# Quantised layer: the third layer's raw query weights are asked for in four groups behind the folding loads of pairs one to four

## The chip, the cores and the metric

The kernel runs on one core of one Trainium2 chip. The metric is the device time in microseconds; the kernel before has a median of 2282.21 us over 3 runs (2281.89 to 2282.95).

## The reference

A chain of four layers, each a gated cross-attention and a gated feed-forward part, on x of 16 x 56 tokens of width 256 (896 tokens, 7 tiles of 128) with a context of 16 x 1500 x 64:

```python
x = x + tanh(g_xattn[n]) * Ln_xattn(layernorm(x), ctx, Wq, w_kc_q, w_kc_kv, W_qr, W_kr, Wo)
x = x + tanh(g_ffn[n]) * Ln_ffn(layernorm(x), ...)
```

The change lies in the feed-forward part of the second layer (n = 1), the quantised one, and concerns weights of the attention of the third (n = 2):

```python
def _L1_ffn_ref(x, w_gate, w_up, w_down, ln_weight):      # bit_linear: x to 8 bits per row, w to -1, 0, 1
    h = silu(bit_linear(x, w_gate)) * bit_linear(x, w_up)  # 896 x 1024
    h = rms_norm(h, ln_weight)
    return bit_linear(h, w_down)

def _L2_xattn_ref(...):                                    # 16 heads, K = 128, D_CQ = 192, R = D_C = 64
    q_hk = (hidden_q @ Wq.T).reshape(Bv, Sv, H, K)
    q_big = apply_rope(einsum('bshk,hkq->bshq', q_hk, w_kc_q))
    q_r = einsum('bshq,hqr->bhsr', q_big, W_qr)
    k_r = einsum('bld,hdr->bhlr', kv_r, W_kr)
    ...
    ctx_lat = einsum('bhsd,hkd->bhsk', ctx_c, w_kc_kv)
    return ctx @ Wo.T
```

## The kernel before

The program is cut into stages that end with a meeting of all five engines (`stage_end`). Each layer is an attention stage, a projection and a feed-forward stage. Inside a stage each engine runs its own program in order and waits on semaphores of the others. SyncE (SP) has no arithmetic: it issues the loads, in the order of its program, and a wait in it holds every load behind it.

The feed-forward stage of the quantised layer works by one list of tasks, `FFN1`, that all engines walk. Its main part goes over the 7 token tiles ("blocks"): `qin` (VectorE, DVE, quantises a tile of the input, L2454), `in` (TensorE, PE, turns it, L1639; ScalarE, ACT, copies it, L2037), `hidden` (PE: gate and up products through the helper at L922; ACT: silu of the gate, `sg`, L2047; DVE: product with up, `h`, L2778), `square` (ACT, L2052; then GpSimd, POOL, multiplies h by `ln_w`, L2237), `rms` (DVE L2792, POOL L2241), `quant` (DVE: maximum L2797, small steps, quantising of h L2454), `turn` (PE L1658, ACT L2057), `down` (PE L922, DVE adds to X, L2783).

Woven into it is the folding of the third layer's weights, head pair by head pair (8 pairs of 2 heads): `fload` (SP: WrT, then WoT and Wv), `fu` (PE, L1181, 8 products; ACT copies to U2, L1709) and `fm` (PE, L1187; ACT to MH, L1712; DVE to ML, L2298). `fold_order(2, 1)` has one set of buffers for the three weights of a pair, so the load of pair p + 1 waits for the products of pair p: SP waits for `fu` of pair p ahead of WrT, and for `fm` of pair p ahead of WoT and Wv. `bit_order` puts `fu` and `fm` of one pair at the end of each block. Thus PE's order in round k is: hidden of block k, down of k - 3, turn of k - 2, in of k + 2, fu and fm of pair k.

The other loads of the stage are issued in `sp_bits`: `ln_w`, the folding loads of pair 0, then eight large ones, `Wq2` (4 x 512 KB) and `Wc2` (4 x 384 KB), the raw query weights and w_kc_q of the third layer in four groups of 4 heads; a group counts on its own semaphore, `heads_in(g)`. Then come the folding loads of pairs 1 to 7. PE waits for `heads_in(g)` in the next stage only, in `pe_rope_queries`, ahead of heads 0, 4, 8 and 12.

Of the kernel before, what the change touches and what calls it, by code (L numbers as in the profile page):

```python
# [432 lines left out]
def build(nc, io, out, steps=8):  # L433
# [494 lines left out]
    def stage_end(e, n):  # L928

        e.drain().then_inc(meet.sem, 1)  # L930
        e.wait_ge(meet.sem, 5 * n)
# [43 lines left out]
    def sp_fold(e, n, p):  # L975
        src = lambda name: io[f"a{n}_{name}"][:, 2 * p:2 * p + 2]
        q = p - FOLD_BUFS[n]
        buf = fold_bufs[n][p % FOLD_BUFS[n]]
        if q >= 0:
            e.wait_ge(*fu_made.at(n, q))  # L980
        e.dma_start(buf["wr"][:, :, :], src("WrT")).then_inc(fold_r.sem(n, p), 16)
        if q >= 0:
            e.wait_ge(*fm_made.at(n, q))
        e.dma_start(buf["wo"][:, :, :], src("WoT")).then_inc(fold_m.sem(n, p), 16)
        e.dma_start(buf["wv"][:, :, :], src("Wv")).then_inc(fold_m.sem(n, p), 16)
        if n == 2:
            return
        if q >= 0:
            e.wait_ge(*fa_made.at(n, q))
        e.dma_start(buf["wq"][:, :, :], src("Wq")).then_inc(fold_a.sem(n, p), 16)  # L990
        e.dma_start(buf["wc"][:, :, :, :], src("WcT")).then_inc(fold_a.sem(n, p), 16)
# [128 lines left out]

    def sp_bits(e):
        e.dma_start(lw[:, :], io["f1_ln"].rearrange("(a n) -> a n", a=1).broadcast_to([P, I1])).then_inc(ln_in.sem(), 16)
        begun = False
        for kind, *t in FFN1:
            if kind == "fload":
                sp_fold(e, *t)
            elif not begun:
                begun = True
                for g in range(4):
                    hs = slice(4 * g, 4 * g + 4)  # L1130
                    e.dma_start(Wq2[g // 2][:, 4 * (g % 2):4 * (g % 2) + 4, :], io["a2_Wq"][:, hs, :]).then_inc(heads_in.sem(g), 16)
                    e.dma_start(Wc2[:, hs, :], io["a2_Wc"][:, hs, :]).then_inc(heads_in.sem(g), 16)
        stage_end(e, next(met))
# [8 lines left out]
    def sync_program(e):  # L1142
        e.dma_start(ident[:, :], io["ident"]).then_inc(ident_in.sem(), 16)
        e.dma_start(X[:, :, :], io["x"].rearrange("b s d -> (b s) d").rearrange("(i p) d -> p i d", p=P)).then_inc(x_in.sem(), 16)
        e.dma_start(gates[:, 0:4], io["g_xattn"].rearrange("(a n) -> a n", a=1).broadcast_to([P, 4])).then_inc(g_in.sem(), 16)
        e.dma_start(gates[:, 4:8], io["g_ffn"].rearrange("(a n) -> a n", a=1).broadcast_to([P, 4])).then_inc(g_in.sem(), 16)
        for tile, name in ((Wq0, "a0_Wq"), (Wk0, "a0_Wk")):
            for r in range(4):
                e.dma_start(quarter(tile, r), heads_of(name, r)).then_inc(fold0_a.sem(), 16)
        e.dma_start(V0[:, :, :], io["ctx"][:, 0:S, :].rearrange("b l d -> l b d")).then_inc(v0_in.sem(), 16)  # L1150
        e.dma_start(mtf[:, :], io["mask_t"]).then_inc(masks_in.sem(), 16)
        e.wait_ge(*fold0_m.at())
        e.wait_ge(*fold0_a.at())
        for k, name in enumerate(("f1_gate", "f1_up", "f1_down")):
            e.dma_start(raws[k][:, :], io[name]).then_inc(wraw_in.sem(k), 16)
        stage_end(e, next(met))
        for n in range(4):
            sp_attention(e, n)
            if n == 1:
                sp_bits(e)  # L1160
            else:
                sp_experts(e, n)
        e.wait_ge(*x_stored.at())
# [1745 lines left out]
```

## Time and profile before

| | us |
|---|---|
| median of 3 runs | 2282.21 |
| profiled execution, first to last instruction (span) | 2276.6 |
| PE busy | 2145.4 |
| DVE busy | 1540.0 |
| POOL busy | 1482.0 |
| ACT busy | 1036.5 |
| feed-forward stage of the quantised layer, first load to first load of the next stage | 861.3 to 932.8 |

Times in the rows are microseconds from the start of the span. A row of a timeline has: start, duration, engine, line of the kernel, operation, output<-input, shape, how many were merged (x), and in brackets the idle time ahead of it with what ended it. PEld is the load of weights into PE. SPq is SP's queue: a row there is the issue of a transfer, not the transfer. A row of stretches has: from:to, length, busy time of PE, PEld, DVE, ACT and POOL with the number of instructions, the TensorE clock that was granted (1.00 is 2.4 GHz, 0.50 is 1.2 GHz), the mean busy share of the 16 DMA engines, and the GB/s that they moved.

### The profile page before, as it was taken

To read this page: it belongs to the slowest core of one execution; us is meant where nothing else is said; L and a number is where in the kernel's file an instruction comes from. 1 tells how busy PE (TensorE), PEld (TensorE's weight loads), DVE (VectorE), ACT (ScalarE), POOL (GpSimd) and SP (SyncE) were. 2 spreads that over 40 slices of the span, in tenths; PEclk is the share of its full clock that TensorE was granted. 3 is DMA by queue.
4 is the path that set the end of the run, shared out by engine and by line. 5 is a ranking of instruction groups with operands and counts; after the bars stand their busy time and mean duration, and the time that the engine had idled before them with its cause. 6 is when DMAs were issued, how large, how long until landed. Compare 5 with 4: busy or idle time off the path is not lost.

```text
span 2276.6 us, 30620 instructions
## 1 busy us (share of the span) xinstructions
PE 2145.4 (94%) x11236; PEld 1519.8 (67%) x11236; DVE 1540.0 (68%) x2492; ACT 1036.5 (46%) x1533; POOL 1482.0 (65%) x933
## 2 busy tenths in 40 slices
PE   7797999999999997898999999979998999999988
PEld 5585777766666664565666666578896666666588
DVE  6766863588888856666787888653335787888653
ACT  4452333555555445212555545434335555545443
POOL 0355763488888873465888888724443888888744
PEclk9798999999999998898999999989999999999989
DMA  3126875211121104001111111025531111111022
GB/s 93 44 74 190 254 239 148 74 42 41 41 61 42 28 29 131 24 1 42 41 42 61 41 41 43 6 84 150 145 85 55 41 42 60 41 42 43 6 65 82
DMA packets 60640, 160.14 MB, mean 70 GB/s; under 512 B 9669, under 2 KB 19669, under 8 KB 60108
## 3 DMA queue, kind: packets, MB, share of 16 engines
q1 hardware_dynamic: 60108, 157.86, 23.2%
q8 instruction: 90, 1.47, 0.3%
q14 instruction: 58, 0.48, 0.1%
q10 hardware_dynamic: 384, 0.33, 0.1%
HBM read 143.18 MB, written 14.98 MB: 69 GB/s over the span
## 4 chain that ended last, share of the span: by engine, by line
PE 83%; DVE 6%; ACT 3%; issue 2%; POOL 2%; DMA 2%; SPq 1%; ACTq 0%; PEldq 0%; DVEq 0%; POOLq 0%; PEld 0%
PE psum L922 21%; PE psum L1426 19%; PE psum L1416 10%; PE psum L1397 10%; PE psum L1418 10%; PE psum L1580 2%; PE psum L1443 2%; PE psum L1537 2%; PE psum L1303 1%; PE psum L1181 1%; POOL CL L1871 1%; DMA WqrT<-in_a_WrT 1%; PE psum L1201 1%; PE psum L1277 1%; ACT E L1849 0%
## 5 line engine op out<-in xcount | busy, mean ns | idle before, releaser
L1849 ACT ACTIVATE E<-psum 125x896 f32<-125x896 f32 x576 | 528.1, 920 | 574.4 <-PE psum L1418 546.9
L2417 DVE TENSOR_REDUCE mx<-psum 128x1 f32<-128x500 f32 x945 | 611.8, 675 | 166.5 <-PE psum L1397 164.5
L2151 POOL TENSOR_TENSOR SA<-SA,E 125x896 f32<-125x896 f32 x282 | 597.4, 2118 | 22.1
L1426 PE MATMUL psum<-E,V 125*64 125x448 f32 x2304 | 472.0, 544 | 0.0
L1416 PE MATMUL psum<-Q,K 128*125 128x448 f32 x1152 | 332.1, 369 | 2.3 <-ACT E L1849 2.3
L1397 PE MATMUL psum<-K,Q 128*128 128x500 f32 x945 | 328.8, 402 | 2.6 <-ACT Q L1836 2.2
L1418 PE MATMUL psum<-Q,K 128*125 128x448 f32 x1152 | 330.3, 368 | 0.0
L1426 PEld LDWEIGHTS psum<-E,V 125*64 125x64 f32 x2304 | 171.6, 136 | 213.9 <-issue 202.5
L2151 POOL TENSOR_TENSOR SA<-SA,SB 125x896 f32<-125x896 f32 x93 | 194.2, 2088 | 148.5 <-DVE SB L2440 148.5
L1397 PEld LDWEIGHTS psum<-K,Q 128*128 128x128 f32 x945 | 174.5, 188 | 134.3 <-issue 34.7
L1416 PEld LDWEIGHTS psum<-Q,K 128*125 128x125 f32 x1152 | 213.2, 187 | 37.0 <-ACT E L1849 6.9
L1418 PEld LDWEIGHTS psum<-Q,K 128*125 128x125 f32 x1152 | 214.8, 186 | 21.8
L2202 POOL TENSOR_TENSOR HL<-HF,HH 128x448 fp32r<-128x448 f32 x70 | 81.2, 1163 | 135.7 <-ACT HH L1957 135.7
L2444 DVE RECIPROCAL RS<-psum 128x448 f32<-128x448 f32 x48 | 142.0, 2958 | 25.4 <-PE psum L1443 25.4
L2440 DVE TENSOR_TENSOR SB<-E,E 125x896 f32<-125x896 f32 x96 | 121.2, 1262 | 28.4 <-ACT E L1849 28.4
L2659 DVE TENSOR_TENSOR HF<-R,psum 128x448 f32<-128x448 f32 x62 | 38.4, 621 | 139.2 <-PE psum L922 122.5
L2151 POOL TENSOR_TENSOR SA<-E,E 125x896 f32<-125x896 f32 x48 | 102.2, 2129 | 46.5 <-ACT E L1849 46.5
L2212 POOL TENSOR_SCALAR S<-slot_of_t,slots 128x896 fp32r<-128x896 bf16 x32 | 91.5, 2864 | 46.3 <-DMA slot_of_t<-slots_scratch 32.1
L2132 POOL TENSOR_TENSOR Q<-QR,Q 64x448 fp32r<-64x448 f32 x96 | 109.5, 1141 | 11.9 <-POOL SA L2151 7.1
L1836 ACT ACTIVATE Q<-QR 64x448 fp32r<-64x448 f32 x192 | 110.5, 575 | 3.7 <-ACTq L930 0.3
L922 PE MATMUL psum<-YH,WH 128*128 128x448 f32 x264 | 104.4, 395 | 2.4 <-DVEq L930 2.4
L922 PE MATMUL psum<-YL,WH 128*128 128x448 f32 x264 | 100.2, 380 | 0.0
(299 smaller groups left out, 3591.5 us busy)
## 6 DMA issues: line engine op xcount, KB each, us to landing
K<-kt_scratch SPq DMA_DIRECT2D x48, 750.0 KB, 4.8
K<-kt_scratch SPq DMA_DIRECT2D x48, 375.0 KB, 6.0
EW<-in_f_w SPq DMA_DIRECT2D x64, 256.0 KB, 8.3
kt_scratch<-kt SPq DMA_DIRECT2D x16, 750.0 KB, 7.7
WS<-in_f_w SPq DMA_DIRECT2D x31, 384.0 KB, 4.6
GB<-gates_scratch SPq DMA_DIRECT2D x36, 224.0 KB, 3.9
slot_of_t<-slots_scratch SPq DMA_DIRECT2D x64, 112.0 KB, 4.8
WoT<-in_a_WoT SPq DMA_DIRECT2D x24, 256.0 KB, 4.2
```

The lines of the kernel that those rows point to most:

```text
L922: i = e.matmul(o, a, b, start=start and n == 0, stop=stop and n == len(pairs) - 1, **kw)
L1397: e.matmul(psum[:, bank, 0:CW], Q1n[b % 3][:, tok(j)], K1t[b % 3][:, c * CW:(c + 1) * CW], start=True, stop=True).then_inc(small_made.sem, 1)
L1416: e.matmul(psum[0:LP, pair + c, 0:HT], K1t[b % 3][:, cols], Q1n[b % 3][:, half[c]], start=True, stop=False)
L1418: i = e.matmul(psum[0:LP, pair + c, 0:HT], K2t[b % 2][:, cols], Q2n[b % 2][:, half[c]], start=False, stop=True)
L1426: i = e.matmul(psum[c * DC:(c + 1) * DC, 4 + b % 2, 0:HT], V[0:LP, b, k * DC:(k + 1) * DC], E[g[n, b, k] % NE][0:LP, half[c]], start=k == ...
L1836: i = e.activation(high, raw, ACT.Copy)
L1849: e.activation(E[m % NE][0:LP, :].rearrange("p (c q) -> p c q", c=2), psum[0:LP, pair:pair + 2, 0:HT], ACT.Exp).then_inc(exp_set.sem, 1)
L2132: e.tensor_tensor(low, raw, high.bitcast(F32), ALU.subtract).then_inc(*(pool_own.up() if odd == 0 else (q2_set.sem, 1)))
L2151: e.tensor_tensor(SA[b % 2][0:LP, :], a[0:LP, :], x[0:LP, :], ALU.add).then_inc(sum_set.sem, 1)
L2417: e.tensor_reduce(mx[:, b % 2, j * 3 + c:j * 3 + c + 1], psum[:, bank, 0:CW], AX.X, ALU.max).then_inc(small_free.sem, 1)
L2440: e.tensor_tensor(SB[list(PAIRED).index(k)][0:LP, :], e0, e1, ALU.add).then_inc(pair_set.sem, 1)
L2444: e.reciprocal(RS[:, :], psum[:, bank, 0:HT]).then_inc(small_free.sem, 1)
```

## The change

SP's walk over `FFN1` still issues the folding loads at the same tasks. The large loads are no longer issued all at once at the first task that is no `fload` (behind pair 0). Group g of them (one `Wq2` and one `Wc2` load) is issued directly behind the folding loads of pair p = g + 1, so behind pairs 1, 2, 3 and 4. Transfers, sizes, buffers and semaphores are the same.

```diff
     def sp_bits(e):
         e.dma_start(lw[:, :], io["f1_ln"].rearrange("(a n) -> a n", a=1).broadcast_to([P, I1])).then_inc(ln_in.sem(), 16)
-        begun = False
         for kind, *t in FFN1:
             if kind == "fload":
-                sp_fold(e, *t)
-            elif not begun:
-                begun = True
-                for g in range(4):
+                n, p = t
+                sp_fold(e, n, p)
+                g = p - 1
+                if 0 <= g < 4:
                     hs = slice(4 * g, 4 * g + 4)
                     e.dma_start(Wq2[g // 2][:, 4 * (g % 2):4 * (g % 2) + 4, :], io["a2_Wq"][:, hs, :]).then_inc(heads_in.sem(g), 16)
                     e.dma_start(Wc2[:, hs, :], io["a2_Wc"][:, hs, :]).then_inc(heads_in.sem(g), 16)
```

## Rows read from the trace of the kernel before

**Rows 1.** The page: its first line, and the chain that ended last by engine.

```profile
span 2276.6 us, 30620 instructions
PE 83%; DVE 6%; ACT 3%; issue 2%; POOL 2%; DMA 2%; SPq 1%; ACTq 0%; PEldq 0%; DVEq 0%; POOLq 0%; PEld 0%
```

**Rows 2.** Three stretches of the quantised layer's stage; columns as told above.

```profile
861.00:869.00 8.00, 6.12 (x22) 3.26 (x22) 3.24 (x12) 3.53 (x5) 0.00 (x0) 0.57 0.83 258
869.00:878.00 9.00, 2.90 (x17) 1.40 (x16) 4.96 (x12) 3.08 (x6) 2.90 (x2) 0.85 0.95 339
878.00:932.00 54.00, 41.58 (x256) 26.92 (x256) 41.72 (x103) 30.61 (x62) 23.26 (x26) 0.87 0.17 52
```

**Rows 3.** Timeline of SP: the last large load, then pair 1's WrT and Wv.

```profile
867.12 0.43 SPq L1132 DMA_DIRECT2D Wc<-in_a_Wc  x1
...
869.12 0.48 SPq L981 DMA_DIRECT2D WqrT<-in_a_WrT  x1
...
870.27 0.43 SPq L985 DMA_DIRECT2D Wv<-in_a_Wv  x1
```

**Rows 4.** Issue to landing: WrT pairs 0-1, WrT 2-7, Wv 2-7, Wc's four.

```profile
DMA to landing us min/median/max: 5.1/6.8/8.6
...
DMA to landing us min/median/max: 2.6/2.7/2.9
...
DMA to landing us min/median/max: 2.5/2.7/3.3
...
DMA to landing us min/median/max: 5.9/7.8/10.0
```

**Rows 5.** Timeline of PE (L1639 in, L1181 fu, L1187 fm, L1658 turn, L922 hidden).

```profile
871.34 0.38 PE L1639 MATMUL psum<-ident,Y 128*128 128x128 f32 x2
877.82 1.51 PE L1181 MATMUL psum<-WqrT 64*96 64x64 f32 x8 [6.10 <-DMA WqrT<-in_a_WrT]
...
882.96 1.04 PE L1658 MATMUL psum<-ident,h 128*128 128x128 f32 x8
...
884.15 0.89 PE L1181 MATMUL psum<-WqrT 64*96 64x64 f32 x8
884.97 0.65 PE L1187 MATMUL psum<-WoT,Wv 128*64 128x256 f32 x4
885.55 1.90 PE L922 MATMUL psum<-wq,xqT 128*128 128x512 bf16 x8
...
889.85 0.89 PE L1181 MATMUL psum<-WqrT 64*96 64x64 f32 x8 [0.44 <-DVE X L2783]
...
905.61 1.14 PE L1181 MATMUL psum<-WqrT 64*96 64x64 f32 x8 [0.54 <-DVE X L2783]
```

**Rows 6.** Timeline of ACT: silu of blocks 2 and 3.

```profile
882.24 1.12 ACT L2047 ACTIVATE sg<-psum,c_gate 128x1024 f32<-128x1024 f32 x1 [0.39 <-PE psum L922]
...
886.98 1.10 ACT L2047 ACTIVATE sg<-psum,c_gate 128x1024 f32<-128x1024 f32 x1
```

**Rows 7.** Timeline of DVE: quantising of blocks 0, 1, 2 (L2454), h of 2, 3 (L2778).

```profile
875.89 0.75 DVE L2454 TENSOR_SCALAR h<-h,h_scale 128x1024 f32<-128x1024 f32 x1
...
883.39 1.28 DVE L2778 SCALAR_TENSOR_TENSOR h<-psum,c_up,sg 128x1024 f32<-128x1024 f32 x1 [2.12 <-ACT sg L2047]
...
887.08 0.75 DVE L2454 TENSOR_SCALAR h<-h,h_scale 128x1024 f32<-128x1024 f32 x1
...
888.12 1.28 DVE L2778 SCALAR_TENSOR_TENSOR h<-psum,c_up,sg 128x1024 f32<-128x1024 f32 x1
...
893.26 2.50 DVE L2454 TENSOR_SCALAR h<-h,h_scale 128x1024 f32<-128x1024 f32 x1
```

**Rows 8.** Timeline of POOL: multiplication by ln_w of blocks 2 and 3.

```profile
887.16 2.90 POOL L2237 TENSOR_TENSOR h<-h,ln_w 128x1024 f32<-128x1024 f32 x1 [1.76 <-ACT sg L2052]
...
892.87 2.34 POOL L2237 TENSOR_TENSOR h<-h,ln_w 128x1024 f32<-128x1024 f32 x1 [0.64 <-ACT sg L2052]
```

**Rows 9.** A stretch behind block 5's start; columns as in rows 2.

```profile
906.00:909.00 3.00, 3.00 (x14) 1.30 (x14) 2.79 (x13) 1.82 (x5) 1.24 (x3) 0.52 0.17 49
```

## Prediction of what the change does to the time

> **What bounds the kernel now.** I read the page first: the span is 2276.6 us, and TensorE (PE) holds 83% of the chain that ended last [rows 1]. The median of the three runs is 2282.21 us, 5.6 us more than this span; the edit touches nothing outside the span, so I work out a difference and take it from the median. Then the three stretches of the quantised layer [rows 2]: in 861 to 869 us the DMA engines are 83% busy, in 869 to 878 us 95% busy while PE works 2.90 of 9 us, and in the remaining 54 us they are 17% busy. So the stage has one place where transfers rule. The queue of SyncE (SP) shows why [rows 3]: the last of the eight large loads goes out at 867.12, and only behind it, at 869.12, the first folding load of pair 1 (WqrT). It lands 8.6 us later, where the six of pairs 2 to 7, which have a quiet queue, take 2.6 to 2.9 [rows 4]. PE, which runs its program in order, ends its last step at 871.34 + 0.38 = 871.72 and stands 6.10 us until that load is there; the profile names it as the releaser [rows 5].
>
> Ahead of this point nothing moves: pair 1's first load waits for the product of pair 0, which PE ends at 869.1 in either version, and pair 0's loads already stand in front of the large ones. The large loads themselves (3.5 MB) are first read in the next stage, behind 932 us, so they have slack of tens of microseconds.
>
> **The change, part by part.**
>
> *Removed: the eight issues between the loads of pairs 0 and 1.* Pair 1's first load goes out at 869.12 as now, since it waits for PE, but now nothing is left in front of it. It then lands at 869.12 + 2.6 to 2.9 = 871.7 to 872.0 [rows 3, 4]. Released 0.1 us after the landing, as now (877.82 against 869.12 + 8.6), its product "fu" starts at about 871.9 instead of 877.82: 5.9 us earlier on PE. The second product of the pair, "fm", starts 0.82 us behind it when warm (884.97 against 884.15) [rows 5], so 872.75; but its last load (Wv, issued at 870.27) takes 2.5 to 3.3 us, median 2.7, and lands at 872.8 to 873.6 [rows 3, 4]. I take 873.1 for fm.
>
> *The clock of PE comes back too.* The stop makes PE restart at half speed: pair 1's fu takes 1.51 us, pair 2's 0.89 [rows 5], and from its start to the ScalarE (ACT) activation of the next block (sg) it is 882.24 - 877.82 = 4.42 us instead of 886.98 - 884.15 = 2.83 [rows 5, 6]: 1.6 us more. Stop and restart together would let block 2 go 5.9 + 1.6 = 7.5 us earlier. That isn't what the stage gains, because VectorE (DVE) becomes late.
>
> *What is late next: DVE and GpSimd (POOL) in block 0's quantising.* DVE quantises block 0 at 875.89, by its own chain, which doesn't move. Now it takes 0.75 us, beside an idle POOL. In block 2 it takes 2.50 [rows 7]: POOL had begun its multiplication by ln_w at 892.87, 0.39 us before DVE's 893.26, and DVE ends at 893.26 + 2.50 = 895.76, 0.55 us after POOL's end at 892.87 + 2.34 = 895.21 [rows 7, 8]. DVE has three such rows (2.2 to 2.6 us) among its seven blocks. Where DVE was first (887.08 against 887.16) DVE keeps its 0.75 and POOL takes 2.90 instead of 2.34. After the change POOL's multiplication of block 1 starts 3.01 us behind fu (887.16 against 884.15), plus what fm is held: 871.9 + 3.01 + 0.35 = 875.3. That is 0.6 us ahead of DVE's 875.89, so DVE should be held: POOL ends at 877.65, DVE at 878.2 instead of 876.64. From there to its product of the next block (h) it needs 0.3 us, with a small copy between (888.12 against 887.08 + 0.75), so h of block 2 starts at 878.5 instead of 883.39 [rows 7]: 4.9 us earlier. Beside this, the Trainium skill ("GPSIMD Engine Reference", section Specifications) says that the two engines share their SBUF interfaces, with contention where a DVE instruction uses two ports; the rows 7 and 8 agree. Without that rule the time would be that of rival A, with it that of my forecast.
>
> *The next block.* PE turns block 0's quantised rows 0.15 us after DVE's end: 878.35, and starts pair 2's fu 1.19 us behind that (884.15 against 882.96): 879.54 [rows 5]. Its sg follows 2.83 us later, 882.37, and lasts 1.12 [rows 6], so h of block 3 can start at 883.5; DVE's own chain, 4.73 us from h to h (888.12 against 883.39), would give 883.2 [rows 7]. So 883.5 against 888.12: 4.6 us earlier. From here each block is a copy of the one before: fu of pair 3 waits for DVE's X (0.44 us) [rows 5], and DVE moves along.
>
> *Added: four times two large loads behind pairs 1 to 4.* Group 0 goes out from 870.75, directly behind Wv. The queue is free from then on: fu of pair 1 ends at about 872.8 and releases pair 2's first load. A group is 896 KB, at the 339 GB/s of the saturated stretch 2.7 us [rows 2], so group 0 is through by about 874.5 and pair 2's first load lands by 877.3 at the latest, 2.2 us ahead of its use at 879.54. Pairs 3 to 5 have longer blocks around them (893.26 - 887.08 = 6.2 us and more from one quantising to the next [rows 7]) and so more slack. An issue takes SP about 0.4 us [rows 3], on a queue that waits for PE anyway: nothing. The last group goes out near 888 us, some 40 us ahead of need: nothing. The waits of SP are the old ones; none is added. So this part is priced 0, with bounds of 0 and of the second rival's price; a gain is excluded because no transfer of this stage is wanted earlier than now, except those of pair 1.
>
> *What takes some back.* With DVE held, PE has nothing from 875.6 (fm at 873.1, block 2's products 0.58 behind it and 1.90 long [rows 5]) to 878.35, and then only small work until block 3's products, 1.40 us behind fu, at 880.9. In the profile the clock is 0.85 of full over the stretch with the long stop and 0.87 over the rest of the stage [rows 2]: pair 5's fu at 905.61 takes 1.14 us and the granted clock is 0.52 in 906 to 909 [rows 5, 9], after a block in which PE had stood for DVE, while in the blocks of pairs 2 and 3 fu takes the warm 0.89. So after such short stops it falls in some blocks only; I take every other. If it falls here, sg of block 3 comes up to 1.6 us later, and some 1.2 if fu has already begun. Half of 1.2, 0.6, goes off: 4.6 - 0.6 = 4.0. Later falls move about in either direction (a slow fu lets DVE go ahead of POOL and saves the 2.50 - 0.75 = 1.75 us of a collision), which I leave at 0 with 1 us to each side.
>
> Sum: 4.0 us, 2282.2 - 4.0 = 2278.2 us.
>
> **The rivals.**
>
> *A. No collision in block 0.* If Wv lands 3.3 us after its issue, the top of its range, fm is 0.5 us later still and POOL starts at 875.8 to 875.9, level with DVE's 875.89. From there on DVE goes first and ends at 876.64. PE turns block 0 at 876.8, fu of pair 2 comes at 878.0, sg at 880.8, h of block 3 at 882.0 instead of 888.12: 6.1 us earlier. Less 0.3 for the clock, 5.8: 2276.4. For it: only 0.6 us separate the two, and large loads follow directly behind Wv. Against: the median landing of 2.7.
>
> *B. The folding loads still wait, now for the group ahead.* If every group held the next pair's load by what the load of pair 1 takes now (8.6 us; the large ones themselves take up to 10.0 [rows 4]), fu of pairs 2 to 5 would follow each other by 8.6 + 0.9 = 9.5 us: 871.9 + 4 x 9.5 = 909.9 for pair 5, against 905.61 now [rows 5], 4.3 us slower, 2286.5. It decides from an average landing of (905.61 - 871.9) / 4 - 0.9 = 7.5 us. Against: 8.6 us came with eight loads in front, not two, and a block's length passes after each group. This is also where the Trainium skill ("DMA: Bandwidth & Descriptors", section Queues, rings and completion order) speaks against the change: each engine consumes a ring's descriptors in order, so a load behind a group waits for all of it. By the row of pair 1 that is true; by my rates it costs no more than the slack.
>
> *C. The gain is mostly given back.* A clock fall in block 2 and one more collision, of block 1 (POOL and DVE were 0.08 us apart there), cost 1.6 and 1.75: 4.6 - 3.3 = 1.3, 2280.9.
>
> **How the numbers follow.** Collision in block 0, with or without a clock fall (gain 3.0 to 5.0): 0.54. Rival A (5.0 to 6.8): 0.26. C (0 to 3): 0.16. B: 0.04. The forecast is the first, 2278.2 us; its own range is 2277.2 to 2279.2. The range for 8 in 10 takes in A's centre and half of C: 2275.9 to 2280.5. A measurement of this kernel can tell about 0.2%, 4.56 us, from no change. Faster than that: A (0.25) and the upper part of the first case (0.14), 0.39. Slower (from B): 0.03. Within: 0.58.
>
> **What would show it.** After: SP issues pair 1's WqrT at 869.1 and it lands in under 3 us; PE's wait for WqrT (6.1 us) is gone and pair 1's fu lasts 0.9 us. POOL's first multiplication of block 1 starts near 875.3 and DVE's quantising of block 0 lasts 2.3 us (A: 0.75). PE stands some 2.7 us for DVE ahead of its first turn of h. The first K load of the next stage goes out 4.0 us earlier against the ln_w load of this one. WqrT of pairs 2 to 5 lands within 4.5 us of issue and nobody waits for it. I am wrong if one of those waits appears, if DVE's quantising stays at 0.75 us, or if the later blocks change their number of collisions (three of seven).

## The result and the profile after

| | before | changed |
|---|---|---|
| median | 2282.47 us (4 runs, 2281.89 to 2282.95) | 2272.38 us (4 runs, 2267.13 to 2275.43) |
| ratio, 95% interval | | 0.9964 [0.9950, 0.9978] |
| span of the profiled execution | 2276.6 us | 2273.6 us (timed at 2275.43) |
| stage of the quantised layer, ln_w issue to rope_q issue | 71.9 us | 66.3 us |

The change is faster by 10 us in these medians and by 8 us in the ratio, where 4.0 was forecast with a range of 1.7 to 6.3. A second comparison further down (12 runs against 29) gives 0.9974 [0.9962, 0.9986], which is 6 us. One execution of e2 took 3064 us at a granted clock of 0.65; it is left out of every median and ratio here.

The same three stretches as in [rows 2] (columns as there), each 1 us later, because ln_w is issued 1.3 us later here; the last one ends, as there, about 1 us ahead of the issue of rope_q:

```profile
862.00:870.00 8.00, 5.44 (x23) 3.12 (x26) 3.19 (x11) 3.60 (x7) 0.00 (x0) 0.58 0.41 123
870.00:879.00 9.00, 6.93 (x32) 3.03 (x32) 5.59 (x14) 5.81 (x11) 4.23 (x3) 0.81 0.70 216
879.00:928.00 49.00, 35.43 (x235) 24.18 (x236) 41.65 (x103) 28.09 (x58) 21.48 (x26) 0.92 0.33 102
```

In the middle stretch PE works 6.93 of 9 us where it worked 2.90, and the DMA engines are 70% busy instead of 95%. The rest is 49 us long instead of 54.

The timeline of PE over the place of the long stop, against [rows 5]:

```profile
872.15 0.38 PE L1638 MATMUL psum<-ident,Y 128*128 128x128 f32 x2
872.88 0.86 PE L1180 MATMUL psum<-WqrT 64*96 64x64 f32 x8 [0.35 <-DMA WqrT<-in_a_WrT]
875.28 0.86 PE L1186 MATMUL psum<-WoT,Wv 128*64 128x256 f32 x4 [1.53 <-DMA Wv<-in_a_Wv]
876.07 2.74 PE L922 MATMUL psum<-wq,xqT 128*128 128x512 bf16 x6
...
879.24 1.04 PE L1657 MATMUL psum<-ident,h 128*128 128x128 f32 x8
```

PE's wait for pair 1's WqrT went from 6.10 to 0.35 us, and its product fu is warm (0.86 us instead of 1.51). But a wait of 1.53 us that the forecast didn't have stands ahead of fm: it is for Wv. These are SP's issues and the landings, against [rows 3, 4]:

```profile
869.93 0.48 SPq L981 DMA_DIRECT2D WqrT<-in_a_WrT  x1
...
871.08 0.43 SPq L985 DMA_DIRECT2D Wv<-in_a_Wv  x1
871.55 0.43 SPq L1130 DMA_DIRECT2D Wq<-in_a_Wq  x1
872.03 0.43 SPq L1131 DMA_DIRECT2D Wc<-in_a_Wc  x1
```

The two landings are, WqrT of pair 1 first, then Wv of pair 1:

```profile
DMA to landing us min/median/max: 2.8/2.8/2.8
...
DMA to landing us min/median/max: 4.1/4.1/4.1
```

Wv has group 0 right behind it (871.55) and takes 4.1 us, not 2.7. WoT, the load between the two (256 KB, issued at 870.52), still lands in 2.7 us. And this is what it does to GpSimd (POOL) and VectorE (DVE), against [rows 7, 8]:

```profile
876.71 0.75 DVE L2453 TENSOR_SCALAR h<-h,h_scale 128x1024 f32<-128x1024 f32 x1
...
877.67 2.35 POOL L2236 TENSOR_TENSOR h<-h,ln_w 128x1024 f32<-128x1024 f32 x1 [2.65 <-ACT sg L2051]
```

POOL's multiplication of block 1 starts 0.96 us behind DVE's quantising of block 0, not 0.6 us ahead of it, and DVE keeps its 0.75 us. That is rival A, by a longer delay than it asked for.

### The profile page after: what moved, and what is told of

It is laid out like the page before. It is cut to its first block, busy times and chain, and to the rows that moved or that the text cites. A ratio compares the mean times of both kernels' runs of the same rounds, so it can differ in the third digit from the quotient of the medians.

```text
span 2273.6 us, 30616 instructions
## 1 busy us (share of the span) xinstructions
PE 2143.3 (94%) x11232; PEld 1518.3 (67%) x11236; DVE 1541.5 (68%) x2492; ACT 1035.6 (46%) x1533; POOL 1478.2 (65%) x933
## 4 chain that ended last, share of the span: by engine, by line
PE 81%; DVE 6%; ACT 3%; POOL 3%; issue 2%; DMA 2%; SPq 1%; ACTq 0%; PEldq 0%; DVEq 0%; POOLq 0%; PEld 0%
PE psum L1425 20%; PE psum L922 19%; PE psum L1415 10%; PE psum L1396 10%; PE psum L1417 10%; PE psum L1442 2%; PE psum L1579 2%; PE psum L1536 1%; PE psum L1302 1%; DMA kt_scratch<-kt 1%; POOL CL L1870 1%; PE psum L1180 1%; PE psum L1200 1%; POOL rstd L2100 1%; PE psum L1276 1%
## 5 line engine op out<-in xcount | busy, mean ns | idle before, releaser
L922 PE MATMUL psum<-YH,WH 128*128 128x448 f32 x264 | 104.1, 394 | 2.4 <-DVEq L930 2.4
L922 PE MATMUL psum<-YL,WH 128*128 128x448 f32 x264 | 99.8, 378 | 0.0
```

The costliest lines, as they stand in the source:

```text
L922: i = e.matmul(o, a, b, start=start and n == 0, stop=stop and n == len(pairs) - 1, **kw)
```

## The experiments

All stage lengths are from the issue of ln_w to the issue of rope_q. "Block 0 held" means that DVE's quantising of block 0 took over 2 us.

### e1: the changed kernel again

No edit.

> The changed kernel once more, to get the size of the effect beside the kernel before on one chip. Stage length below means the issue of the ln_w load to the issue of the rope_q load (71.9 us before, 66.3 us in the profile of the changed kernel). Theory 1 (all of the gain is made in the quantised layer's stage, the rest is drift between executions): the stage again 66 to 68 us, the total 4.5 to 6 us below before, 2276 to 2278 us. Theory 2 (the change also moves something outside the stage): the total 8 to 12 us below before, 2270 to 2274 us, with a second place in the trace where the two timelines move apart by over 2 us.

Measured: 2274.71 us against 2281.15 (12 and 29 runs), 0.9974 [0.9962, 0.9986], 5.9 us. Stage 65.8 us, 6.1 less than the first trace of before. By ratio and stage that is theory 1 (its 2276 to 2278 us were a little too high). What differs outside the stage differs between executions of the same instructions. SP issues ln_w at 857.3 us here, 4 us earlier than in the trace of before, with no changed instruction ahead of it; the 29 runs of before reach from 2273.97 to 2290.23. The four runs that the forecast started from (within 1.1 us of each other) showed nothing of that spread, so part of the first 10 us is probably drift; the eight traces at the end say how much can be told.

### e2: all eight large loads behind pair 7

```diff
-                g = p - 1
-                if 0 <= g < 4:
+                for g in range(4 if p == 7 else 0):
```

> All eight large loads behind the folding loads of pair 7, so that no large load runs while pairs 1 to 7 are fetched. In the changed kernel Wv of pair 1 landed late (PE waits 1.5 us for it) because group 0 came right behind it; that wait set GpSimd's multiplication of block 1 (877.67) behind VectorE's quantising of block 0 (876.71). Here Wv should land in 2.7 us, GpSimd should start 1.5 us earlier, 0.5 us ahead of VectorE. Collision theory: VectorE's quantising of block 0 lasts over 2 us instead of 0.75, block 2 gains nothing, stage 66 to 67.5 us, total within 1.5 us of the changed kernel. Rival (VectorE is not held there and the late Wv was a plain loss): the stage 1.5 us shorter than the changed kernel's, about 64.8 us.

Measured: 2278.28 us, 0.9985 [0.9973, 0.9997]; stage 72.4 us. Wv of pair 1 landed in 2.6 us and block 0 was held:

```profile
874.89 2.27 DVE L2452 TENSOR_SCALAR h<-h,h_scale 128x1024 f32<-128x1024 f32 x1
```

POOL had begun at 874.27. So the collision of the forecast exists, at its predicted place, and h of block 2 comes 17.3 us behind ln_w, 4.8 us earlier than before (forecast 4.9). The stage is 5 us longer than the upper end of what I expected, though, and the total 3.6 us above e1's instead of within 1.5. Behind the collision PE stands 2.75 us and then runs cold (from the timeline of PE):

```profile
877.31 1.38 PE L1656 MATMUL psum<-ident,h 128*128 128x128 f32 x8 [2.75 <-DVE h L2452]
...
879.04 1.54 PE L1179 MATMUL psum<-WqrT 64*96 64x64 f32 x8
880.51 1.12 PE L1185 MATMUL psum<-WoT,Wv 128*64 128x256 f32 x4
881.56 3.45 PE L922 MATMUL psum<-wq,xqT 128*128 128x512 bf16 x8
```

Block 3's products take 3.45 us instead of 1.90 [rows 5], and h of block 3 comes 25.0 us behind ln_w, only 1.9 us earlier than before. From h of block 2 to h of block 3 the forecast had 5.0 us without a clock fall, and here it is 7.7: the fall that I had priced at 0.6 us (half of 1.2) took 2.7.

### e3: all eight behind pair 1

```diff
-                g = p - 1
-                if 0 <= g < 4:
+                for g in range(4 if p == 1 else 0):
```

> All eight large loads behind the folding loads of pair 1: pair 1 is fetched in a quiet queue, pair 2 behind 3.5 MB. If the queue is served in order, the WrT of pair 2, issued some 4 us behind pair 1's, lands 8 to 9 us after its issue, near 883 us by the times of the changed kernel, 2 to 3 us after PE wants it: PE stands there 2 to 3 us for it, and the stage is 2 to 3 us longer than the changed kernel's (68.5 to 69.5 us), still 2 to 3.5 us shorter than before. Rival (small loads are not held by the ones ahead): landing under 5 us and the stage as in the changed kernel, 66 to 67 us.

Measured: 2281.48 us, 0.999 [0.9976, 1.0005]; stage 75.3 us. The WqrT of pair 2 lands 9.6 us after its issue and PE waits for it:

```profile
886.05 1.51 PE L1179 MATMUL psum<-WqrT 64*96 64x64 f32 x8 [5.78 <-DMA WqrT<-in_a_WrT]
```

The queue holds a small load behind eight large ones, at pair 2 as at pair 1: the stall has only moved. I had expected a stop of 2 to 3 us; SP was busy with its own eight issues until 876.2, so WqrT went out 2.3 us later than I had counted. The stage missed its 68.5 to 69.5 us by 6 and is no shorter than before's. The longer wait is 3 us of that; behind it PE restarts at half speed (fu 1.51 us), which I had not counted, and in block 5 stands 3.60 us for DVE once more. The 3.5 MB in one piece ahead of a folding load are the cause of the stop: behind pair 7 (e2), with no folding load to follow, they caused none.

### e4: the changed kernel, and POOL waits for DVE

```diff
                 if i == 0:
                     e.wait_ge(*ln_in.at())
                 e.wait_ge(*ss_set.at(i))
+                if i > 0:
+                    e.wait_ge(*hq_set.at(i - 1))
```

> The changed kernel, with one wait more: GpSimd's multiplication of block i by ln_w starts only when VectorE has quantised block i - 1. VectorE's three quantisings that lasted 2.5 us (blocks 2, 3, 4) should take 0.75 us. Theory (the collision of the two engines is on the path): 1.75 us for each of the three, less what the later GpSimd costs; GpSimd then ends 2.35 us behind VectorE's quantising, 0.8 us ahead of VectorE's next maximum, so nearly all stays: the stage 4 to 5 us shorter, 61.5 to 62.5 us. Rival (another engine is late then, the silu of the next block above all): under 1.5 us.

Measured: 2269.15 us, 0.9945 [0.9927, 0.9963] to before; stage 60.4 us, with all seven quantisings at 0.75 us. One of them and POOL's start right behind its end:

```profile
882.59 0.75 DVE L2455 TENSOR_SCALAR h<-h,h_scale 128x1024 f32<-128x1024 f32 x1
...
883.49 2.37 POOL L2238 TENSOR_TENSOR h<-h,ln_w 128x1024 f32<-128x1024 f32 x1 [2.58 <-DVE h L2455]
```

The stage is 5.9 us shorter than the changed kernel's 66.3 us, more than the 4 to 5 us expected and 0.6 us more than three collisions at 1.75 us; the blocks no longer leave PE such long gaps, and in this trace its clock doesn't fall in any of pairs 1 to 7 (fu 0.86 to 0.89 us throughout).

### e5: the kernel before again

> The kernel before once more, as a measure of how far two executions of the same program differ and for a second trace of its stage. Ratio 1.000 within 0.0015. If the stall is a property of the program, PE waits again 6 us for the WqrT of pair 1 and the stage (issue of ln_w to issue of rope_q) is 71 to 73 us; if the stage of the first trace was an unlucky one, 68 to 70 us.

Measured: 1.0003 [0.9992, 1.0014]; stage 72.6 us, PE waits 6.82 us for pair 1's WqrT. The stop is a property of the program, and a ratio of this study is good to 0.1 to 0.2% (the intervals reach 0.0011 to 0.0018 to each side).

### e6: the kernel before, and POOL waits for DVE

The edit of e4 in the kernel before.

> The kernel before with the wait of e4 alone (GpSimd's multiplication of block i after VectorE's quantising of block i - 1). If the collision and the stall are separate terms, the three held quantisings go back to 0.75 us, the 8.6 us landing of pair 1's WqrT stays, and the stage is 4 to 6 us shorter than before, 66 to 68 us; the large loads' move is then worth the same 5.5 to 6 us on top (e4: 60.4 us). If the collision had only filled time that the stall leaves, it is worth under 2 us here.

Measured: 2274.05 us, 0.997 [0.9958, 0.9981]; stage 66.1 us; PE still waits 6.50 us for WqrT. Collisions and stop are separate terms: without the collisions the move of the large loads is worth 66.1 - 60.4 = 5.7 us.

### e7: groups behind pairs 2 to 5

```diff
-                g = p - 1
+                g = p - 2
```

> The changed kernel with the four groups behind pairs 2 to 5 instead of 1 to 4, so that nothing follows Wv of pair 1. The forecast's own case: Wv lands in 2.6 us (3.1 to 4.1 us in the three runs with a group right behind), GpSimd starts 0.6 us ahead of VectorE, VectorE's quantising of block 0 lasts 2.3 us, h of block 2 comes 17.3 us behind the ln_w load (e2: 17.3; changed kernel 17.0 and 16.1), PE stands 2.7 us for it, and in part of the executions its clock falls. Stage 67 to 70 us, total 0.5 to 3 us above the changed kernel. Rival (the long stage of e2 came from its 3.5 MB behind pair 7): stage 66 us, as the changed kernel.

Measured: 2277.44 us, 0.9988 [0.9977, 0.9999]; Wv in 2.6 us, block 0 held (2.22 us), stage 72.4 us, every block within 0.1 us of e2's. So e2's length didn't come from its 3.5 MB at the end, and my 67 to 70 us missed the clock again: the granted clock (the column ahead of the last two) of e7 behind the collision was

```profile
881.00:887.00 6.00, 6.00 (x22) 2.83 (x21) 3.38 (x9) 3.65 (x7) 2.27 (x2) 0.50 0.45 119
```

half speed for six microseconds.

### e8: groups behind pairs 2 to 5, and POOL waits for DVE

The edits of e7 and e4.

> e7 and e4 together: groups behind pairs 2 to 5, and GpSimd held until VectorE has quantised. If the only reason why a quick Wv didn't pay was the collision, it now costs nothing: h of block 2 15.2 to 15.6 us behind ln_w as in e4 (there VectorE itself is the bound), the stage 60 to 61.5 us, total as e4, 10 to 12 us below before. If the group behind pair 1 had a use of its own, 2 us longer than e4.

Measured: 2266.47 us, 0.9947 [0.993, 0.9965]; stage 60.4 us, the h of each block within 0.1 us of e4's. With the order fixed, the quick Wv (2.5 us) costs nothing and gains nothing. So the group behind pair 1 has no use of its own but the delay of Wv. This is, with e4, the fastest kernel of this study, 12 us below before.

### e9: e7, with the wait of e4 in block 1 only

```diff
                 e.wait_ge(*ss_set.at(i))
+                if i == 1:
+                    e.wait_ge(*hq_set.at(0))
```

> e7 (groups behind pairs 2 to 5, Wv of pair 1 quick) with one wait in one block: GpSimd's multiplication of block 1 waits for VectorE's quantising of block 0; all other blocks are free to collide as before. In e7 this one collision put PE's stop of 2.7 us into block 2, and the clock fell behind it: stage 72.4 us. If that collision is what decides between 66 and 72 us, the stage is 65 to 66.5 us here, with quantisings of 2.5 us in three later blocks as in the changed kernel, and the total 5 to 7 us below before. If it only cost its 1.6 us, the stage is 70 to 71 us.

Measured: 2275.27 us, 0.9976 [0.9961, 0.9991]; stage 69.9 us. Block 0 was free (0.75 us) and h of block 2 came 15.0 us behind ln_w, but the collision came back one block on:

```profile
882.62 2.53 DVE L2455 TENSOR_SCALAR h<-h,h_scale 128x1024 f32<-128x1024 f32 x1
...
882.26 2.35 POOL L2238 TENSOR_TENSOR h<-h,ln_w 128x1024 f32<-128x1024 f32 x1 [1.32 <-ACT sg L2051]
```

The total, 5.5 us below before, is what I expected of the theory, but the stage isn't: 69.9 us belongs to the rival. The order in block 0 does decide the next step: h of block 3 comes 22.3 us behind ln_w, where e7 had 25.0: PE's stop is 1.2 us instead of 2.7 and its clock doesn't fall behind it (fu of pair 2 takes 0.89 us). But this one order doesn't decide the length of the stage. A block that is won makes PE and ScalarE (ACT) earlier, and POOL with them, and the next block may collide instead.

### e10 to e14: more traces of the same programs

e10 is e7 again, e11 to e13 are the changed kernel, e14 is the kernel before.

> e7 once more for its trace. If the fall of PE's clock behind the collision comes in some executions only, the stage is 68 to 70 us here in about every other case; if it always comes, 72 to 73 us again, as in e7 and e2.

> The changed kernel once more for its trace. Wv of pair 1 lands 3.1 to 4.1 us after its issue, VectorE's quantising of block 0 takes 0.75 us, the stage is 65.5 to 66.5 us. If Wv should land under 3 us here, the block collides and the stage is 70 us or more.

> The changed kernel's stage took 66.3, 65.8 and 70.2 us in three traces. The third had a warm-clock fall ahead of pair 0's products and Wv of pair 1 landing in 3.0 us, and VectorE's quantising of block 0 was held (2.55 us). If the order of GpSimd and VectorE in block 0 decides, this trace belongs to one of two groups: block 0 quantised in 0.75 us and a stage of 65.5 to 67 us, or in over 2 us and a stage of 68.5 to 72.5 us.

> As for e12: 0.75 us and 65.5 to 67 us, or over 2 us and 68.5 to 72.5 us. A stage of 68 us or more with block 0 at 0.75 us and no later change of the order would speak against the collision as the cause.

> The kernel before: pair 1's WqrT lands 8 to 9 us after its issue, PE waits 6 to 7 us, and the stage takes 71 to 73 us (71.9 and 72.6 us in two traces), since PE's stop is longer than the difference between the two orders.

| trace | landing of pair 1's Wv, us | quantising of block 0, us | stage, us |
|---|---|---|---|
| changed, first | 4.1 | 0.75 | 66.3 |
| e1 | 3.4 | 0.75 | 65.8 |
| e13 | 4.3 | 0.75 | 67.7 |
| e11 | 3.0 | 2.55 | 70.2 |
| e12 | 2.7 | 2.31 | 68.8 |
| e2 | 2.6 | 2.27 | 72.4 |
| e7 | 2.6 | 2.22 | 72.4 |
| e10 | 2.7 | 2.26 | 68.7 |
| before, e5, e14 | 8.3, 8.9, 9.1 | 0.75 | 71.9, 72.6, 73.8 |

These two lines are the ones that tell an execution in which Wv came early, here e11 (DVE, then POOL, which was 0.34 us ahead):

```profile
874.75 2.55 DVE L2453 TENSOR_SCALAR h<-h,h_scale 128x1024 f32<-128x1024 f32 x1
...
874.41 2.34 POOL L2236 TENSOR_TENSOR h<-h,ln_w 128x1024 f32<-128x1024 f32 x1 [1.35 <-ACT sg L2051]
```

In e1 it was closer still on the other side, DVE at 871.57 and POOL at 871.69. So the stages of the changed kernel fall into two groups, by which of two engines starts first in block 0: 65.8 to 67.7 us in three traces, 68.8 and 70.2 in two. In the eight rows above that of before, and in e3 (3.7 us, free), a landing of 3.0 us or less goes with a held block 0, one of 3.4 us or more with a free one. In all nine DVE starts block 0's quantising 6.8 us behind the issue of pair 1's WqrT, so DVE is a fixed mark; POOL starts 6.1 to 6.4 us behind that issue where block 0 is held and 6.9 to 8.3 where it is free. It is the landing of Wv that moves POOL across the mark.

e13 is 0.7 us over the 67 us that I gave its group. Like the other two it has three held blocks, but its third is block 5 (2.06 us) instead of block 4, and PE stands 3.60 us for it and turns the last block at half speed (1.94 us instead of 1.06). e10 repeats e7's program and is 3.7 us shorter. Of this, 0.9 us stood already ahead of the collision, where pair 0's fu was cold in e7 (1.35 us) and not in e10 (0.89); at h of blocks 3 to 5 the two are still 0.8 to 1.0 us apart, and the rest comes behind, where e7 has a collision in block 5 with a stop of 3.60 us. e11 missed its expectation, which had taken a Wv of over 3.1 us for certain, and e14 was 0.8 us over its 73 us, with a landing of 9.4 us for WqrT.

The times of h behind ln_w show where the two groups part:

| h, us behind ln_w | changed, block 0 free (first, e1, e13) | block 0 held (e2, e7, e10 to e12) | e9 | e4, e8 |
|---|---|---|---|---|
| block 2 | 17.0, 16.1, 17.1 | 16.4 to 17.6 | 15.0 | 15.5 |
| block 3 | 21.9, 21.4, 22.0 | 24.1 to 25.3 | 22.3 | 21.0 |

At block 2 they are level: the late Wv costs there what the collision costs. They part in the next step, in which PE stands 2.7 us and runs at half speed only where block 0 was held.

## Why the prediction was right or wrong

**The stop and what stands behind it: right.** Pair 1's WqrT lands in 2.8 us (forecast 2.6 to 2.9), the 6.1 us wait is 0.35, and fu is warm. In the same trace DVE then becomes the late engine, as said. The Trainium skill's rule on the queues ("DMA: Bandwidth & Descriptors", section Queues, rings and completion order) agrees with the 9.6 us of e3; in the changed kernel its cost, rival B, didn't come: the WqrT of pairs 2 to 6 landed in 2.6 to 4.6 us in the first trace, and pair 2's in 4.5 to 5.5 us over the five, later than the 4.5 us that I had allowed; PE waited for none.

**The landing of Wv: wrong, and this is the step that failed.** It reads "its last load takes 2.5 to 3.3 us, median 2.7" and took the median. That row holds the landings of a queue with nothing behind the load. With group 0 issued 0.47 us behind, the six traces that have large loads directly there (five of the changed kernel and e3) gave, with e4 as a seventh, 2.7 to 4.3 us; the five traces without (e2, e7 to e10) gave 2.5 to 2.7. I had priced "added: four times two loads" at 0 and excluded a gain; its first group delayed a load by up to 1.6 us, and this delay put POOL behind DVE. That the load in front, and not only the one behind, is held was not in my sum; it stands only as an argument for rival A ("large loads follow directly behind Wv"), without a price. The delay gains nothing by itself (block 2 is no earlier for it). What it saves is PE's stop and the half clock behind it: the stages with block 0 free are 2.9 us shorter in the mean than the two with it held. These are only five traces. e9, which fixed the order alone, shows 2.7 us against e7 and 1.8 against e10 at h of block 3, but nothing sure at the end of the stage (69.9 us against 72.4 and 68.7).

**The collision: mechanism right, likelihood wrong.** Where Wv was quick it happened at the named place with the named price: quantising 2.2 to 2.6 us (forecast 2.3), h of block 2 in e2 and e7 17.3 us behind ln_w, 4.8 us earlier (forecast 4.9), PE's gap 2.73 to 2.75 us (forecast 2.7). Where Wv was slow, rival A's stage came: the three traces have a mean of 66.6 us against 72.8 for the three of before, 6.2 us less (rival A: 5.8). I gave the first case 0.54 and A 0.26; it was two of five and three of five. The Trainium skill's line on the shared interfaces ("GPSIMD Engine Reference", section Specifications) agrees with e4, whose edit only makes one of the two engines wait for the other, and in which all seven quantisings took 0.75 us; that this collision is the one of a DVE instruction with two ports, no run here shows.

**The clock: under-sized.** I charged 0.6 us for a fall behind the collision, by "every other" and 1.2. It came in all five traces with block 0 held: fu of pair 2 took 1.54 us in each. My "every other" came from stops of 1.88 us. The trace of before had a longer one, in block 5, which I didn't use, and it had the fall behind it:

```profile
918.59 1.06 PE L1658 MATMUL psum<-ident,h 128*128 128x128 f32 x8 [3.60 <-DVE h L2454]
...
919.81 1.54 PE L1181 MATMUL psum<-WqrT 64*96 64x64 f32 x8
```

The two held traces of the changed kernel have a mean stage of 69.5 us, 3.3 us below before, where my case said 4.0; e2 and e7 gained nothing in their traces. This error made the forecast too large for its own case, so it hid a part of the miss: the stage gained more than forecast only because the other case came in three of five.

**The measured size.** The mean stage of the changed kernel over five traces is 67.8 us, of before over three 72.8: 5.0 us. The two ratios give 8.2 us [5.0, 11.4] and 5.9 us [3.2, 8.7]. The stage's 5.0 us lie inside the second and at the lower edge of the first. In the same eight traces the part from the issue of rope_q to the end takes 1344.0 us changed and 1344.2 before, in the mean, so nothing moved there. ln_w is issued at 861.3 us changed and 862.9 before, with the same instructions ahead of it and 857.3 to 864.3 us as the range. So the failed step and the clock together explain 1.0 us of the miss, the difference of 5.0 and 4.0 (1.6 in the first profiled execution, whose stage is 5.6 us shorter). The rest of the first comparison I put down to the spread of executions; that is argued and not shown, and which share of the 8.2 us it made up is open. The forecast's range was made of its cases alone and had no term for this spread, of which its three runs (1.1 us) showed nothing.

## What to carry to other kernels

Large loads with slack belong behind small ones that an engine is about to wait for, in pieces short enough for one round of the loop: 3.5 MB in one piece cost PE 6 us at pair 1 and again at pair 2 (e3), and four pieces of 0.9 MB cost it between nothing and 1.5 us, for the small load just ahead of them. When the forecast of a gain hangs on which of two engines starts first by half a microsecond, price both orders, give each its chance, and look for the wait that fixes the order: here one wait on GpSimd in every block was worth more than the change itself: 66.1 us of stage against a mean of 72.8 (e6), where the move of the loads gave 5.0 us in the mean. The same wait in one block alone only moved the collision on (e9). Take the landing time of a load from a row in which the same kind of load stands behind it, too.

## What the runs showed of the hardware

- A load of 64 KB landed later with larger ones issued 0.47 us behind it: 3.0 to 4.3 us in four of five traces of the changed kernel (2.7 in the fifth), 2.5 to 2.7 us in the five traces (e2, e7 to e10) without them. The 256 KB load issued 1.0 us ahead of the group kept its 2.7 to 2.8 us.
- GpSimd's multiplication of 128x1024 and VectorE's tensor-by-scalar step on another block of the same size exclude each other: the one that comes second waits. VectorE's 0.75 us became 2.06 to 2.62, ending about 0.55 us behind GpSimd's end; GpSimd's 2.35 us became up to 2.93 where VectorE was first. VectorE's product h, of the same size but with one input in PSUM, kept its 1.28 us beside a running multiplication (before: 888.12, inside GpSimd's 887.16 to 890.06).
- After gaps of 2.7 us, with small products behind them, the granted clock fell to half in all five traces of this kind and stayed there for six to seven microseconds (e7: 0.50 over 881 to 887). After the stops of 3.60 us in block 5, the fu behind took 1.54 us in five of six traces (before, e2, e3, e7, e9) and 1.31 in the sixth (e13).
- Executions of one program spread by 16 us (before, 29 runs: 2273.97 to 2290.23), although a set of four lay within 1.1 us.
